# Cross-attention and gated FFN on one NeuronCore: the W12 products of three of the four FFN blocks as Strassen's seven products

## The reference

```python
x = x + xattn(layernorm(x), ctx, ctx, w_q, w_k, w_v, w_out, mask)
# the FFN on h = layernorm(x):
x12 = h @ w12.T + b12            # w12 is 2048 x 1024
x1, x2 = split(x12, 2)
x  = x + (silu(x1) * x2) @ w3.T + b3
```

## Time and profile before

| | us |
|---|---|
| median of 3 runs (1115.88 to 1122.79) | 1116.13 |
| the profiled execution | 1120.0 |
| its span | 1118.2 |
| PE matmul busy, share of the span | 1068.1, 96% |
| DVE / ACT / POOL busy | 570.7 / 425.9 / 393.8 |
| granted TensorE clock, mean | 0.991 |
| output stage of block 0, hidden stage of block 1 | 699.5 to 741.0, 741.0 to 823.9 |

### The profile page before, as it was taken

How to read it: one execution, slowest core, us unless ns; L and a number is a source line. 1 busy time by engine, 2 the same in 40 slices (tenths; PEclk the granted TensorE clock), 3 DMA queues, 4 the chain that set the end, 5 groups by cost and what they waited for, 6 DMA issues and landing times.

```text
span 1118.2 us, 19298 instructions
## 1 busy us (share of the span) xinstructions
PE 1068.1 (96%) x7888; PEld 646.4 (58%) x7888; DVE 570.7 (51%) x1062; ACT 425.9 (38%) x899; POOL 393.8 (35%) x376
## 2 busy tenths in 40 slices
PE   5887899999999989999999999999999999999998
PEld 3776766867668667686655544444444444444443
DVE  6878777776676766577645423631134111431121
ACT  5757545555556546455566510111110111011100
POOL 2769701513415124157685788112000300121000
PEclk8999999999999999999999999999999999999999
DMA  9558596897988968569784643370006400360001
GB/s 377 198 130 187 143 255 166 206 213 183 253 189 208 224 178 201 126 165 251 179 239 76 159 180 138 90 243 1 1 2 143 158 1 1 76 188 1 1 1 75
DMA packets 201511, 162.23 MB, mean 145 GB/s; under 512 B 162640, under 2 KB 172880, under 8 KB 196560
## 3 DMA queue, kind: packets, MB, share of 16 engines
q1 hardware_dynamic: 201424, 161.01, 54.0%
HBM read 93.87 MB, written 27.26 MB: 108 GB/s over the span
## 4 chain that ended last, share of the span: by engine, by line
PE 77%; DVE 12%; ACT 4%; DMA 2%; issue 1%; DVEq 0%; ACTq 0%
PE bank_dense L984 70%; DMA arena_attn<-arena_attn 2%; ACT arena_attn L816 2%; DVE arena_in L1349 2%; PE bank_score L1045 2%; PE bank_score L1041 2%; DVE arena_rows L1321 1%; DVE arena_in L1352 1%; DVE arena_in L1262 1%; DVE arena_rows L1310 1%; PE bank_av L1063 1%; PE bank_dense L1001 1%; PE bank_av L1067 1%; DVE arena_in L1366 1%; PE bank_av L1065 1%
## 5 line engine op out<-in xcount | busy, mean ns | idle before, releaser
L984 PE MATMUL bank_dense<-arena_rows,arena_in 128*128 128x256 f16 (+1 forms) x2304 | 348.1, 309 | 4.0 <-DVE small L1224 1.4
L984 PEld LDWEIGHTS bank_dense<-arena_rows,arena_in 128*128 128x128 f16 x2304 | 223.8, 98 | 112.4 <-DVE small L1224 1.7
L816 ACT ACTIVATE arena_attn<-bank_score,arena_in 128x128 f32<-128x128 f32 x512 | 192.8, 467 | 154.9 <-DVE arena_in L1352 154.9
L984 PE MATMUL bank_dense<-arena_out,arena_attn 128*128 128x512 f16 x768 | 172.2, 382 | 0.0
L984 PE MATMUL bank_dense<-arena_attn,arena_rows 128*128 128x512 f16 x768 | 166.4, 379 | 0.0
L984 PE MATMUL bank_dense<-arena_out,arena_in 128*128 128x512 f16 x768 | 166.1, 379 | 0.0
L1401 DVE SCALAR_TENSOR_TENSOR arena_attn<-bank_dense,small,arena_attn 128x512 f32<-128x512 f32 x32 | 24.0, 750 | 221.9 <-PE bank_dense L984 221.9
L702 POOL TENSOR_TENSOR arena_attn<-arena_attn 128x512 f16<-128x512 f32 x53 | 63.7, 1201 | 200.5 <-ACT arena_attn L825 200.5
L984 PEld LDWEIGHTS bank_dense<-arena_out,arena_in 128*128 128x128 f16 x768 | 75.0, 98 | 90.9 <-issue 0.4
L984 PEld LDWEIGHTS bank_dense<-arena_attn,arena_rows 128*128 128x128 f16 x768 | 75.1, 98 | 90.7
L658 POOL TENSOR_TENSOR small<-small 128x1 f32<-128x1 f32 x32 | 24.1, 755 | 290.9 <-DVE small L1304 290.9
(11 more groups left out here) (122 smaller groups left out, 1306.7 us busy)
## 6 DMA issues: line engine op xcount, KB each, us to landing
arena_rows<-x SPq DMA_DIRECT2D x32, 512.0 KB, 6.0
arena_attn<-q_scratch SPq DMA_DIRECT2D x48, 256.0 KB, 4.6
arena_rows<-w_t SPq DMA_DIRECT2D x12, 1024.0 KB, 6.2
arena_rows<-ctx_t SPq DMA_DIRECT2D x8, 1024.0 KB, 5.9
q_scratch<-arena_attn SPq DMA_DIRECT2D x16, 512.0 KB, 5.5
x_scratch<-arena_rows SPq DMA_DIRECT2D x16, 512.0 KB, 3.9
arena_out<-x_scratch SPq DMA_DIRECT2D x16, 512.0 KB, 6.1
out<-arena_out SPq DMA_DIRECT2D x16, 512.0 KB, 3.7
```

The lines of the kernel that those rows point to most:

```text
L816: ins = act.activation(e[:, g % 2, u, SEQ * j:SEQ * j + SEQ], B_SCORE[g % 2][:, SEQ * h:SEQ * h + SEQ], ACT.Exp, bias=neg_max[:, g % 2, h: ...
L984: ins = pe.matmul(dst, lhs(a, c), rhs(b, c), start=(c == 0 and n == 0), stop=(c == KC - 1 and n == 2))
```

## The change

**The algorithm.** For blocks 1 to 3 two chunk pairs (m1, m1 + 4) of the same kind k (x1 or x2) form one unit; UNITS = 8 units a block, in the order of `unit_of(i)`: pair i // 2, kind i % 2. A unit is a 2 x 2 product: W12's rows in halves (m1, m1 + 4), the 1024 inputs in halves, the 512 tokens in halves. Strassen's formulas make it of NP = 7 products instead of 8, each of 4 input chunks x 3 matmuls of 256 columns. `LEFT` lists the seven combinations of W12's quarters (five sums, two plain quarters), `RIGHT` those of the rows' quarters (again five sums).

**Weights.** W12 is loaded again unit by unit (`load_raw`, two DMAs of 512 KB). POOL makes the five sums (`weight_sums`, 128x512 f32, two buffers `w_sum`), ACT the seven high pieces (`unit_w_hi`), DVE the seven low ones (`unit_w_lo`) into a ring of SLOTS = 4 units of 14 KB a partition. Each unit is stored to DRAM (`store_unit`, 1.8 MB); blocks 2 and 3 load it back (`load_unit`) three units ahead. Chunks m and m + 4 now share their scale (`in_pairs`: two small DVE instructions in the attention).

**Rows.** Two row tiles at a time (tiles 0 and 2, then 1 and 3 of a block): statistics, root and normalising as before, then POOL's five sums (`row_sums`, two buffers `y_sum`), ACT's seven high and DVE's seven low pieces, and four transposing DMAs (`turn_rows`). There is one buffer `yq` for the turned rows instead of two.

**Combining.** `B_SEVEN` are the five PSUM banks that the attention has left. ACT copies products 0, 1, 2 of a unit to SBUF (`keep`), DVE combines the rest in eight instructions of 256 elements (`mix`); then Silu, gate and the hidden pieces as before, on SBUF.

**Where it stands in the orders.** PE (f >= 1): `seven_products(f, i)` takes the place of `hidden`. It waits for the unit's low pieces (block 1) or its load, for the turned rows and, for product j, for the reader of the product five before.

```diff
@@ DVE, from the last residual of the attention on
             residual(NB - 1, 2)
             residual(NB - 1, 3)
+            for r in range(2):
+                row_stats(2 * NB + FT + r)
+            for r in range(2):
+                normalise(2 * NB + FT + r)
...
                 first_half_read(0, m)
                 gate(0, m)
                 hid_lo(0, m)
+            rows_lo(1, 0)
             dve.wait_ge(s_b3, 16)
             dve.wait_ge(s_yres, 64)
             for u in range(FT):
                 ins = dve.tensor_tensor(y_res[:, u], y_res[:, u], b3_all, ALU.add)
             ins.then_inc(s_yresb, 1)
             for f in range(NF):
+                r = 2 * NB + FT * (f + 1)
+                for i in range(UNITS if f else 0):
+                    mix(f, i)
+                    if f == 1 and i <= 4:
+                        unit_w_lo(i + 3)
+                    if f + 1 < NF and i == 5:
+                        row_stats(r)
+                        row_stats(r + 1)
+                    if f + 1 < NF and i == 6:
+                        normalise(r)
+                        normalise(r + 1)
                 if f:
-                    for m in range(MC):
-                        first_half_read(f, m)
-                        gate(f, m)
-                        hid_lo(f, m)
+                    for n in range(2):
+                        unit_hid_lo(f, 3, n)
+                if 1 <= f < NF - 1:
+                    rows_lo(f + 1, 0)
                 for q in range(8):
+                    if f + 1 < NF and q == 1:
+                        row_stats(r + 2)
+                        row_stats(r + 3)
+                    if f + 1 < NF and q == 2:
+                        normalise(r + 2)
+                        normalise(r + 3)
+                    if f + 1 < NF and q == 4:
+                        rows_lo(f + 1, 1)
+                    if f == 0 and q >= 5:
+                        unit_w_lo(q - 5)
                     ffn_residual(f, q)
@@ DVE, new
+            def unit_w_lo(i):
...
+                    dve.wait_ge(s_uhi, NP * i + j + 1)
+                    dve.scalar_tensor_tensor(out=ring[:, i % SLOTS, j, 1], in0=src, scalar=scale("w_in", unit_of(i)[0]),
+                                             in1=ring[:, i % SLOTS, j, 0], op0=ALU.mult, op1=ALU.subtract)\
+                       .then_inc(s_ulo, 1)
@@ POOL
             prob_lo(NG - 1)
-            for k in range(4):
+            for k in range(3):
                 split_w3(k)
+            root(2 * NB + FT)
+            root(2 * NB + FT + 1)
+            row_sums(1, 0)
+            split_w3(3)
             for f in range(NF):
...
+                if f == 0:
+                    for i in range(UNITS):
+                        weight_sums(i)
...
+            def weight_sums(i):
+                pool.wait_ge(s_raw[raw_at(i)], 32 * (i // 2 + 1 - raw_at(i) // 2))
+                for n, j in enumerate(LEFT_SUMS):
+                    n += len(LEFT_SUMS) * i
+                    if n >= 2:
+                        pool.wait_ge(s_ulo, lo_of_sum(n - 2, LEFT_SUMS))
+                    add(w_sum[:, n % 2], LEFT[j], lambda m, k: weight_quarter(i, m, k), s_wsum)
@@ ACT
+            rows_hi(1, 0)
             for f in range(NF):
+                for i in range(UNITS if f else 0):
+                    v, p = UNITS * (f - 1) + i, i // 2
+                    keep(v, 0)
+                    if i % 2:
+                        unit_silu(f, p, 0)
+                    keep(v, 1)
+                    if i % 2:
+                        unit_silu(f, p, 1)
+                    elif p:
+                        unit_hid_hi(f, p - 1, 0)
+                    keep(v, 2)
+                    if i % 2 == 0 and p:
+                        unit_hid_hi(f, p - 1, 1)
+                    if f == 1 and i <= 4:
+                        unit_w_hi(i + 3)
...
                 if f + 1 < NF:
-                    for u in range(FT):
-                        rows_hi(2 * NB + FT * (f + 1) + u)
+                    rows_hi(f + 1, 1)
+                if f == 0:
+                    for i in range(3):
+                        unit_w_hi(i)
@@ PE
+                for j in range(NP):
...
+                    if last >= 0 and last % NP < 3:
+                        pe.wait_ge(s_kept, 3 * (last // NP) + last % NP + 1)
+                    elif last >= 0:
+                        pe.wait_ge(s_mixed, 4 * (last // NP) + last % NP - 2)
...
+                    for c in range(4):
+                        for n, (a, b) in enumerate(((0, 0), (0, 1), (1, 0))):
+                            ins = pe.matmul(seven(v, j), ring[:, v % SLOTS, j, a, P * c:P * c + P], rows_of(j)[:, b, c],
+                                            start=(c == 0 and n == 0), stop=(c == 3 and n == 2))
+                    ins.then_inc(s_seven, 1)
```

More of the change, by code:

```diff
@@ new lines, in unit_w_hi @@
+            def unit_w_hi(i):
+                done_sums = 0
+                if i >= SLOTS:
+                    act.wait_ge(s_seven, NP * (i - SLOTS + 1))
+                    act.wait_ge(s_ustore[i % SLOTS], 16)
+                else:
+                    act.wait_ge(s_dense, done("h", 0, MC - 1, 1))
+                act.wait_ge(s_raw[raw_at(i)], 32 * (i // 2 + 1 - raw_at(i) // 2))
+                for j in range(NP):
+                    if j in LEFT_SUMS:
+                        at = len(LEFT_SUMS) * i + done_sums
+                        done_sums += 1
+                        act.wait_ge(s_wsum, at + 1)
+                        src = w_sum[:, at % 2]
+                    else:
+                        src = weight_quarter(i, *LEFT[j][0])
+                    act.activation(ring[:, i % SLOTS, j, 0], src, ACT.Copy, scale=scale("w_in", unit_of(i)[0]))\
+                       .then_inc(s_uhi, 1)
@@ new lines, in keep, with unit_silu @@
+            def keep(v, j):
+                act.wait_ge(s_seven, NP * v + j + 1)
+                if v == 0 and j == 0:
+                    act.wait_ge(s_w3, 16)
+                elif v:
+                    act.wait_ge(s_mixed, 4 * (v - 1) + (2 if j == 2 else 1))
+                act.activation(kept[j], seven(v, j), ACT.Copy).then_inc(s_kept, 1)
+            def unit_silu(f, p, n):
+                v, m = UNITS * (f - 1) + 2 * p, p + 4 * n
+                act.wait_ge(s_mixed, 4 * v + 3 + n)
+                act.activation(both[:, 0, n], both[:, 0, n], ACT.Silu, bias=b12[:, m:m + 1], scale=c_hid[:, m:m + 1])\
+                   .then_inc(s_silu, 1)
@@ L775, in x_hi, with unit_hid_hi @@
+            def unit_hid_hi(f, p, n):
+                m = p + 4 * n
+                act.wait_ge(s_gated, MC * f + 2 * p + n + 1)
+                if p == 0 and n == 0:
+                    act.wait_ge(s_dense, done("y", f - 1, 7))
+                act.activation(hid[:, 0, m], both[:, 1, n], ACT.Copy, scale=hid_scale[:, m:m + 1]).then_inc(s_hhi, 1)
             def x_hi(r, h):
@@ L977, in spread_top, with product @@
                 pe.matmul(dst[:, 0:2 * k], ones[0:k, :], diag[0:k, :, 0:k], start=True, stop=True).then_inc(ready, 1)
-            def product(dst, lhs, rhs, before=None):
-                for c in range(KC):
+            def product(dst, lhs, rhs, before=None, chunks=range(KC)):
+                for c in chunks:
                     if before:
```

334 lines of the change are left out of this document (266 added, 68 removed).

## The result

The changed kernel takes **1147.49 us** in the median of four runs (1146.5 to 1149.05), the kernel before, run beside it, 1117.61 us (1115.88 to 1122.79). The ratio is 1.026, with a 95% interval of 1.023 to 1.029: slower. The profiled execution has a span of 1144.7 us against 1118.2.

The account below looks back on a forecast made before the run. The FFN was taken to be bound by PE's matmul columns. Block 1 +48, blocks 2 and 3 -19, output stages +1.4, b3 +2: +32.4 on 1118.2, span 1150.6; plus 1.8, less 3.9: 1148.5, rounded 1149 us; range 1110 to 1172.

Parts of the forecast that it names:

- Matmuls, -9.5 a block: Hidden stages of blocks 1 to 3: 672 matmuls of 256 columns at 109.2 ns, 73.4 us a block instead of 82.9.
- Unit costs: Combining a unit: ACT 2.7 us, DVE 4.9 us, both fitting into PE's 9.2 us.
- Border, +15.8: Output stage of block 0 with splitting of unit 0: block 1's hidden stage starts at 756.7, not 741.0.
- The second term: At the border of block 0, PE waits from 720.8 for the first residual, done at 727: +6.2 us.
- A split unit, 9.3 us: Block 1, splitting one unit's weights on POOL, ACT and DVE: 9.3 us, between 6.5 without turns and 9.9.
- Units 1 and 2 until 778, PE idle 14 us: Start of block 1: splits and residuals keep DVE and ACT until 778; PE makes five products, then idles 14 us.
- 14.2 us a unit, end at 872: Block 1 from 778: five units at mix 4.8 + split 9.3 + 0.1, against PE's 9.2; end at 872, +48.
- Blocks 2 and 3: Hidden stages with units loaded from DRAM: -9.5 us each, -19; POOL's b3 beside the mixes costs 2 us in all.
- The terms of +0.7: Output stages 1 and 2: the second pair of tiles is loaded late, residual 1 ends 21.4, wanted at 20.7: +0.7 each.
- No turns: Rival: DVE and POOL don't wait for each other, 11.5 us a unit in block 1; 1115.5 us, chance 0.13.
- That the splits hide: Rival: in block 1 DVE never waits for a sum or high piece, split unit under about 6.5 us; 1095, chance 0.09.
- Strict lock and slow clock: Rival: split unit 9.9 us, 15.3 a unit in block 1, PE's clock falls after waits; 1163, to 1172, chance 0.21.

Follow-up runs that it names:

- Experiment 4: Changed kernel with the splits, loads and stores of units 3 to 7 left out, output not the reference's: 1.010; with SP's loads moved behind the transposes, 1122.04 us, 1.002.
- experiment 1: Changed kernel with four buffers instead of two for POOL's weight sums: 1144.87 us, ratio 1.022 to the kernel before.
- experiment 2: Changed kernel with the five weight sums of each unit made by DVE instead of POOL: 1142.67 us, ratio 1.021 to the kernel before.
- experiment 3: Changed kernel with weight sums on DVE and POOL's b3 of block 1 behind the last low piece: 1136.08 us, ratio 1.016 to the kernel before.
- experiment 6: Changed kernel with block 1 back on eight products, units split meanwhile for blocks 2 and 3 through five ring buffers, sums on DVE: 1124.63 us, ratio 1.006.
- experiment 8: Block 1 on eight products, units split meanwhile for blocks 2 and 3, 512 KB transfers spread between piece stores: 1109.87 us, ratio 0.992 to the kernel before.

## Why the prediction was right

The forecast was 1149 us and 1147.5 was measured. Its steps:

- **Matmuls, -9.5 a block**: 674 matmuls in 73.40 us. Right, and with it the rate of 109.2 ns from the earlier trace rows. (The row at 57.26 isn't a second product of 24, as the prediction has it, but a single small matmul; it starts when the 24 before it have been issued, so the rate stands.) The rule of the Trainium skill that was weighed there (TensorE: Matmul & The Clock Gate, section Back-to-back issue gap), by which the change would have lost here, disagrees with this trace too.
- **Unit costs**: copies of `keep` 0.36 to 0.38 us, `mix` 3.4 and two instructions of 0.75; DVE has 40.71 us in the eight units of hidden 2, 5.1 a unit with the statistics. Experiment 4 shows that PE stays fed by this.
- **Border, +15.8**: +15.1. hid_lo(0, 7) let PE go on at 709.80 (forecast 709.8), W3's last quarter at 732.52 (732.5), unit 0 at 756.13 (756.7). The second term was mis-split: the stand for residual 0 was 3.05 us, not 6.2, because PE was slower before it. 51 matmuls took 13.52 us after the first stand, where 11.0 are due, at a lower clock; DVE was the bound in both accounts.
- **A split unit, 9.3 us**: 9.0 in four of the five units (780.86 to 789.82), 10.1 in the last, beside b3. The 9.3 was chosen between 6.5 and 9.9 and not summed, so the closeness is in part luck; but both mechanisms are in the trace. In the unit from 780.86, two sums lengthen the low pieces by 2.0 us (3.43 instead of 1.41), and DVE then stands 1.91 us, up to 788.84, for ACT's high piece of the last sum, which is the chain. Experiments 1, 2 and 3 tell the terms apart: four sum buffers shorten the first two units by 2 us each and nothing in the end; sums on DVE bring 1.3 to 1.6 us in the units of experiment 2 that b3 doesn't touch (12.6 to 11.3, 13.6 to 12.2, 14.4 to 12.8), although DVE's own work grows by 3.4. The two trade places: with the wait gone in experiment 1, a third sum falls on the low pieces (3.08 us for three at 785.23), so they can't be added up as separate savings. The Trainium skill (SBUF — State Buffer, section SBUF: two separate sides) calls this an exclusive lock; by the rows at 782.18, 790.08 and 847.55 the trace agrees that such instructions hold each other up, but not for the whole instruction: a sum of 1.27 us adds 1.0 us to the low pieces or `mix` beside it. A unit was 0.9 us shorter than the strict turns of the rival (9.9): two sums fell on the low pieces, not three, and one fell into DVE's wait.
- **Units 1 and 2 until 778, PE idle 14 us**: first `mix` at 777.46, PE idle for 11.85 us. `keep` ends the stand before `mix` starts, which I hadn't allowed for; it changes nothing behind it.
- **14.2 us a unit, end at 872**: the `mix` starts at 777.46 and 847.55, five units apart, make 14.0. End at 869.12, 2.9 us early.
- **Blocks 2 and 3**: -9.5 and -9.6. The terms of +0.7 for output 1 and 2 were 0 and 0.4, the 2 us for POOL's b3 didn't show: no stand in either hidden stage.

The sum was 5.9 us too high on the span (1150.6 against 1144.7: 2.9 from hidden 1, 1.0 from the output stages, 2.0 from b3). The median came out within 1.5 us of the forecast because another term was off the other way: I took the profiled execution to be 3.9 us above the median, as before; this time it was about 1 us below (1144.7 + 1.8 = 1146.5). So the stage times bear the forecast out, and a part of the closeness of the total is luck.

**The rivals.** No turns: refuted by the rows at 782.18 and by experiment 1, where the low pieces take 3.43 us with no chain before them. That the splits hide: refuted, a split unit costs 9.0 us and not 6.5; even with no splits beside the products (experiment 4) the kernel is at 1.002. Strict lock and slow clock: the clock did fall, 0.87 in hidden 1, and PE was busy 85.09 us for 73.4 us of matmuls, but the period stayed at 14.0 us and not 15.3, as DVE and its chain with POOL set it and PE had room (in these five units DVE waited for PE once, 0.64 us).

## What to carry to other kernels

Fewer columns on TensorE pay in full only where the engines that prepare them have slack; count those engines' work at the first use, not in the steady state. Here the saving of 9.5 us a block was real, and the block in which the weights are split lost almost five times as much (45.2, border included); splitting for later blocks beside a block that runs the old way turned the loss into a gain of 0.8%. Sums that "idle" GpSimd takes over aren't free beside VectorE's instructions with two SBUF inputs: moving five of them to the busier VectorE made a unit 1.3 to 1.6 us shorter. Size a staging ring for the longest burst that its DMA queue can hold ahead of it, or spread the burst: spreading took hidden 1 from 94.5 to 91.2 us.

## What the runs showed that I had not expected

- POOL's sum is 1.27 us alone and 1.7 beside DVE's low pieces, sum after sum (five in 8.54 in experiment 1), while the low pieces pay more: 3.43 us for two instead of 1.41. Of the time lost in turns, DVE takes the larger part. Beside POOL's 128x1024 instructions two low pieces took 5.58 us (experiment 2).
- The clock didn't follow the length of the last stand alone. In output 0 PE stood 3.05 us and ran its next 24 matmuls of 512 columns in 5.35 us, full speed; in hidden 1 it stood 2.10 us, after stands of 2.72 and 11.85 shortly before, and needed 4.46 us for 24 of 256 columns, where 2.78 is full speed.
- A store of 256 KB lands in 3.0 us in the median of experiment 6 and in 4.3 in that of experiment 8, but stores queued behind six loads of 512 KB held ACT for 11.7 us (experiment 6).
